# One fused audio-tower kernel: round two's results of token pairs 6 and 7 picked by TensorE from weight tables, and half of the shared experts moved forward

## The chip, the cores and the metric

The kernel runs on one core of one Trainium2 chip. The metric is device time in microseconds (us) of one execution. Five engines run their own instruction streams and meet at semaphores: TensorE (PE in the profile, its weight loads PEld), VectorE (DVE), ScalarE (ACT), GpSimd (POOL) and SyncE (SP), which here only issues DMAs.

## What is computed

Three layers on 64 batches x 16 positions = 1024 tokens of width 128, all in 32-bit floats:

```
h   = einsum("bg,egp->bep", x, weight * mask) + bias      # x: 64 x 5000, weight: 16 x 5000 x 128
h   = h + attention(layernorm(h))                         # 8 heads, causal over the 16 positions
xf  = layernorm(h)
s   = sigmoid(xf @ gate_w.T); top-2 of 64 experts; weights = s / sum(s) * 2.5
y_e = (silu(buf_e @ w1_e) * (buf_e @ w3_e)) @ w2_e         # tokens sent to expert e, at most 256
out = h + sum over the 2 chosen experts of weight * y + silu(xf @ sw1) * (xf @ sw3) @ sw2
```

The last term is the shared experts, which every token passes.

## The kernel before

The 1024 tokens are eight "pairs" of 128 (two positions of all 64 batches), numbered 0 to 7. The first stage streams 40 MB of weights through a ring of 12 buffers; VectorE and GpSimd multiply them by the mask, TensorE sums them (`sum_genes`, L843). Attention of pair j follows two pairs behind. After the last pair is summed, three pairs' attention is still to be finished; in the code that follows the loop `j, k, l` are the pairs 5, 6 and 7.

The experts work on slots. Tokens are scattered by indirect DMA (`scatter`, L486) into a DRAM table of expert inputs, SyncE loads that back (`load_slots`, L399), and 12 groups of 512 slot rows go through: `turn_xs` (transpose, L989 for round one, L993 for round two), `copy_xsT`, `up` (L1015), `silu` (with `copy`, L704/L705), `mid` (on GpSimd for groups 0 to 7, L508; on VectorE for 8 to 11, L1411), `turn_mid` (L1029), `copy_midT`, `down` (L1045), `copy_y` (L715) into `ys`. Groups 0 to 7 are round one (pairs 0 to 4), groups 8 to 11 round two (pairs 5 to 7; 32 slots per expert, 2048 rows). The last pair, 7, is not scattered: VectorE marks its slots (`mark_slots`, L1361/L1362, into `hot`) and TensorE adds its rows onto the transposed group with a 512-column matmul (`add_last`, L999).

`store_group` (L405, SyncE) writes each group's results to DRAM, and GpSimd's `gather` (L533, two indirect DMAs per pair, one for each of the two experts) reads every token's two rows back into `yg`: pairs 0 to 4 once all eight stores of round one have landed, pairs 5, 6, 7 once the four stores of round two have. `combine` (L1429, L1430) multiplies by the router's weights and adds them to `hres`, which by then holds h plus the shared experts' part. `write_out` (L430) stores the output, two DMAs for two pairs at a time, as `s_fin` counts up.

The router's weights of pairs 5 to 7 come from an exponential on ScalarE (`score_exp`, L725) and six small VectorE instructions (`weights`, L1417 to L1422), between `combine(3)` and `combine(4)`. The shared experts are done in two halves of 512 tokens after the last `down`: `shared_up` (two 512-column matmuls, L1056), `silu_shared` (L721), `shared_mid` (L1400), `shared_down` (four 128-column matmuls, L1064), `add_shared` (L1405).

Order is written out by hand: every engine has one program order, and a semaphore wait holds back all that stands behind it on that engine. On TensorE the stretch between the streaming loop and the experts is (L1067 on) `spin`s (dummy matmuls, L928), `turn_qk(k)`, `qkv(k)`, `turn_o(j)`, `values(k)`, `attend(j)`, `turn_xn(l)`, `turn_xs(0)`, `project(l)` (L865), spins and `turn_xs(1)`, `turn_xs(2)`, `up(0)`, `up(1)`, `turn_xs(3)`, `turn_qk(l)` (L869), `turn_xf(j)`, `turn_xs(4)`, `qkv(l)`, `gate(j)` and so on. On ScalarE: `copy_xnT(l)`, `copy_xsT(0)`, `copy_xsT(1)`, `square_qk(l)`, `norm_qk(l)`, `probs(k)`, `copy_xsT(2)`, `norm_xf(j)`, `copy_xsT(3)`, `turned_qk(l)` (L619), `copy_xfT(j)`, `silu(0)`, `heads_k(l)` (its last copy is L630), `silu(1)`, ... On VectorE `choose(j)` (L1336 to L1338), which waits for `gate(j)`, is followed by `multiply_keys(l)` (L1262), which waits for `heads_k(l)`.

Of the kernel before, what the change touches and what calls it, by code (L numbers as in the profile page):

```python
# [27 lines left out]
P = 128  # L28
# [20 lines left out]
GATHERED_EARLY = NCH1  # L49
# [50 lines left out]
def S_BANK(i):  # L100

    return ((1, 5, 7), (0, 2, 3))[i]
# [69 lines left out]
def tower_kernel(nc, x, tok_w, tok_b, tok_mask, W_dq, W_uq, W_qr, W_dkv, W_ukv, W_kr, W_o,  # L172
                 q_ln_g, q_ln_b, kv_ln_g, kv_ln_b, gate_w, w1, w3, w2, sw1, sw3, sw2, consts, masks, out):
    with ExitStack() as ctx:
# [8 lines left out]

        bank = [ctx.enter_context(nc.psum_tensor(f"bank{i}", [P, 512], F32)) for i in range(8)]
# [45 lines left out]
        wts = sb("wts", [P, NCH, 2])  # L230
        msel = sb("msel", [P, NCH, E], BF16)
# [21 lines left out]
        ssil, shs = ring_view(18304, 512), ring_view(18816, 512)  # L253

        hm = [mask[:, 256 * i:256 * (i + 1)].rearrange("p (i h) -> p i h", h=H) for i in range(2)]
        gt = [mask[:, 512 + 256 * i:768 + 256 * i].rearrange("p (i h) -> p i h", h=H) for i in range(2)]
        slot_iota, hot = xT[:, 0:M_SLOTS], prod[:, 0:M_SLOTS]
# [62 lines left out]
        s_iota, s_hot = sem("slot_iota_in"), sem("last_slots_marked")  # L320

# [31 lines left out]
        def _(sp):  # L353
            for j in range(NCH):
                for q in range(UNITS):
# [14 lines left out]
                    if j == 1 and q == UNITS - 1:  # L370
# [9 lines left out]
                        sp.dma_start(gw[0:E, :], gate_w).then_inc(s_tw, 16)  # L380
            sp.wait_ge(s_xTp, 5)
# [31 lines left out]
            load_w2(0, (0, WREM), (0, S))  # L413
            sp.dma_start(slot_iota, masks[:, M_W:M_W + M_SLOTS]).then_inc(s_iota, 16)
            sp.dma_start(sw13[:, 0, :], sw1).then_inc(s_sw, 16)
            sp.dma_start(sw13[:, 1, :], sw3).then_inc(s_sw, 16)
            sp.dma_start(sw2s, sw2).then_inc(s_sw, 16)
            for g in range(STORED_FIRST):
                store_group(g)
# [3 lines left out]
            for g in range(STORED_FIRST, GROUPS):  # L423
                store_group(g)
# [20 lines left out]
        def _(pool):  # L445
            pool.memset(half[:], -0.5).then_inc(s_pool, 1)
            pool.memset(zeros, 0.0).then_inc(s_zsrc, 1)
            pool.wait_ge(s_ones, 1)
# [67 lines left out]
            root_h2(j)  # L516
            mid(0)
            mid(1)
            mid(2)
# [6 lines left out]
            scatter(k)  # L526
            root_h2(l)
            mid(7)

# [8 lines left out]
            pool.wait_ge(s_slot, NCH - 1)  # L538
# [3 lines left out]
            pool.wait_ge(s_ys, GROUPS)  # L542
            for j in range(GATHERED_EARLY, NCH1):
                gather(j)
            pool.wait_ge(s_gidx, 1)
            pool.wait_ge(s_yout[1], 16 * (GROUPS - GROUPS1))
            for j in range(NCH1, NCH):
                gather(j)

        @block.scalar  # L550
        def _(act):
# [95 lines left out]
            def copy_xfT(j):  # L647
                act.wait_ge(s_xfT, j + 1)
                act.copy(xfT[:, P * j:P * j + P], bank[A_BANK(j)][:, 256:384]).then_inc(s_xfTs, 1)
# [72 lines left out]

            def score_exp(first, last):
                act.wait_ge(s_top, last)
                act.activation(ew[:, 0, first:last], top[:, first:last, 0:2], ACT.Exp, scale=-1.0).then_inc(s_exp, 1)  # L725
# [10 lines left out]
            copy_xnT(l)  # L736
            copy_xsT(0)
            copy_xsT(1)
            square_qk(l)
# [8 lines left out]
            heads_k(l)  # L748
            silu(1)
            heads_v(l)  # L750
            copy_oT(k)
# [37 lines left out]
            copy_xsT(9)  # L789
            copy_y(8)  # L790
            silu(9)
# [10 lines left out]
            silu_shared(0)  # L802
            silu_shared(1)
            score_exp(NCH1, NCH)
# [13 lines left out]
        def _(pe):  # L818
# [163 lines left out]
            def turn_xs(g):  # L982
# [37 lines left out]
            def turn_mid(g):  # L1020
                pe.wait_ge(s_hm, g + 1)
                if g >= 1:
                    pe.wait_ge(s_hT, g if g <= GROUPS1 else g - 1)
                if g == GROUPS1:
                    pe.wait_ge(s_kv, 2 * NCH)
# [7 lines left out]
            def down(g):  # L1033
# [3 lines left out]
                if g == 0:  # L1037
                    pe.wait_ge(s_w2, 16 * 4)
                if g >= 1:
# [10 lines left out]
            def shared_up(i):  # L1050

                if i == 0:
                    pe.wait_ge(s_sw, 48)
                    pe.wait_ge(s_hm, GROUPS)
# [500 lines left out]
```

## Time and profile before

| | us |
|---|---|
| runs | 239.67, 241.01, 241.49 (median 241.01) |
| the profiled execution | 241.4 |
| its span, first to last instruction | 239.7 |
| busy PE / DVE / ACT / POOL | 184.3 / 152.4 / 82.7 / 145.6 |
| granted TensorE clock, mean of the span | 0.953 |

Times of the trace count from the span's start. Busy shares are averages over a streaming stage (to some 157 us), a stretch of attention and experts side by side (to some 220 us) and a tail of DMAs, and say little of any one of them. "SPq" and "POOLq" are instructions that issue DMAs. A bracket at the end of a timeline row is the idle time of that engine just before it and what ended that.

### The profile page before, as it was taken

How to read it: one execution, taken by the hardware profiler on the slowest of the kernel's cores; microseconds unless marked ns; L12 is line 12 of the kernel's file. 1: busy time of each engine (PE TensorE's matmuls, PEld its weight loads, DVE VectorE, ACT ScalarE, POOL GpSimd, SP SyncE). 2: the span in 40 equal slices, each digit the busy share in tenths (PEclk: the TensorE clock that was granted, in tenths of full speed). 3: DMA queues.
4: the chain of work that ended last, by engine and by line, in shares of the span. 5: the costliest groups of instructions: out<-in, count | busy, mean ns of one | idle time of the engine just before them, and what ended most of it. 6: DMA issues, size and time to landing. Idle time of an engine off the chain costs nothing.

```text
span 239.7 us, 6216 instructions
## 1 busy us (share of the span) xinstructions
PE 184.3 (77%) x2549; PEld 154.8 (65%) x2549; DVE 152.4 (64%) x366; ACT 82.7 (35%) x245; POOL 145.6 (61%) x117
## 2 busy tenths in 40 slices
PE   0057969558989969979879789699997989999700
PEld 0056949457878958857758767588776767767400
DVE  0024384686497796897996994978999627410571
ACT  2005200003324324324133124136878744344400
POOL 3326469519998949879969949620161651375360
PEclk9999997977999989999999999999999999999975
DMA  6989999999999999999999999949901329234241
GB/s 220 290 311 417 362 419 384 346 421 415 421 413 417 420 418 420 414 427 418 403 408 228 234 218 191 153 87 303 263 0 44 115 68 296 68 98 121 71 112 35
DMA packets 32982, 65.12 MB, mean 272 GB/s; under 512 B 2874, under 2 KB 25367, under 8 KB 32375
## 3 DMA queue, kind: packets, MB, share of 16 engines
q1 hardware_dynamic: 31416, 59.47, 75.0%
q10 hardware_dynamic: 576, 3.26, 3.4%
q0 software_dynamic: 960, 1.97, 3.1%
q8 instruction: 21, 0.34, 0.6%
q14 instruction: 9, 0.07, 0.1%
HBM read 56.96 MB, written 7.73 MB: 270 GB/s over the span
## 4 chain that ended last, share of the span: by engine, by line
PE 32%; DVE 24%; DMA 18%; SPq 9%; ACT 6%; issue 5%; POOL 3%; POOLq 1%; DVEq 0%; ACTq 0%
DMA ring<-in_L_tok_weight_dram 16%; PE bank L843 10%; DVE ring L1241 5%; SPq L362 4%; DVE bank L1271 4%; PE bank L1045 3%; DVE prod L1262 3%; PE bank L1015 3%; DVE prod L1293 2%; DVE bank L1301 2%; SPq L368 2%; PE bank L993 2%; PE bank L999 2%; PE bank L928 2%; POOL rstd L455 2%
## 5 line engine op out<-in xcount | busy, mean ns | idle before, releaser
L466 POOL TENSOR_TENSOR ring<-ring,mask 128x896 f32<-128x896 f32 (+1 forms) x48 | 91.5, 1935 | 18.7 <-DMA ring<-in_L_tok_weight_dram 18.6
L843 PE MATMUL bank<-ring,xT 128*64 128x128 f32 x1248 | 84.3, 294 | 11.3 <-DVE ring L1241 8.0
L843 PEld LDWEIGHTS bank<-ring,xT 128*64 128x64 f32 x1248 | 76.4, 149 | 16.0 <-DVE ring L1241 12.8
L1241 DVE TENSOR_TENSOR ring<-ring,bank 128x1024 f32<-128x1024 f32 (+1 forms) x45 | 45.8, 1049 | 35.4 <-DMA ring<-in_L_tok_weight_dram 35.4
L455 POOL TENSOR_TENSOR rstd<-mv,half 128x1 f32<-128x1 f32 (+1 forms) x24 | 14.4, 603 | 32.4 <-DVE mv L1249 21.5
L533 POOL DMA_INDIRECT ring<-expert_outputs,slot_index x16 | 16.2, 1010 | 16.6 <-DMA expert_outputs<-ring 12.4
L824 PE MATMUL bank<-cst,w 64*128 64x64 f32 x39 | 5.3, 328 | 15.6 <-DMA w<-in_x_dram 14.8
L486 POOL DMA_INDIRECT expert_inputs<-xf,slot_index x14 | 14.3, 1022 | 4.3 <-issue 3.5
L508 POOL TENSOR_TENSOR mask<-ring,mask 128x256 f32<-128x256 f32 x8 | 7.5, 938 | 14.4 <-ACT ring L705 11.4
L824 PEld LDWEIGHTS bank<-cst,w 64*128 64x128 f32 x39 | 5.0, 219 | 15.7 <-issue 14.8
L579 ACT ACTIVATE offset<-shift,rstd 128x1 f32<-128x1 f32 x16 | 4.7, 292 | 25.1 <-POOL rstd L455 25.1
L1015 PE MATMUL bank<-w,ring 128*64 128x128 f32 (+1 forms) x256 | 12.9, 277 | 0.5 <-ACT ring L705 0.4
L1045 PE MATMUL bank<-w2p,ring 64*64 64x128 f32 (+1 forms) x256 | 12.8, 272 | 0.3 <-ACT ring L715 0.2
L1271 DVE TENSOR_REDUCE bank<-prod 128x16 f32<-128x288 f32 (+7 forms) x8 | 12.1, 1511 | 0.3
L1015 PEld LDWEIGHTS bank<-w,ring 128*64 128x64 f32 (+1 forms) x256 | 10.1, 123 | 2.6 <-ACT ring L696 1.1
L1045 PEld LDWEIGHTS bank<-w2p,ring 64*64 64x64 f32 (+1 forms) x256 | 10.2, 120 | 2.3 <-issue 1.2
L1293 DVE TENSOR_TENSOR prod<-vcat,bank 128x256 f32<-128x256 f32 (+7 forms) x8 | 10.8, 1344 | 0.0
L1301 DVE TENSOR_REDUCE bank<-prod 128x128 f32<-128x256 f32 (+7 forms) x8 | 10.6, 1321 | 0.0
L1262 DVE TENSOR_TENSOR prod<-kcat,bank 128x256 f32<-128x256 f32 (+5 forms) x6 | 6.5, 1089 | 4.8 <-ACT vcat L635 4.8
L1336 DVE MAX8 top<-bank 128x8 f32<-128x64 f32 x8 | 1.9, 232 | 12.0 <-PE bank L914 12.0
L715 ACT COPY ring<-bank 128x512 f32<-128x512 f32 x12 | 7.0, 585 | 7.0 <-PE bank L1045 7.0
L928 PE MATMUL bank<-cst 128*128 128x128 f32 x70 | 9.4, 279 | 0.0
(153 smaller groups left out, 297.4 us busy)
## 6 DMA issues: line engine op xcount, KB each, us to landing
ring<-in_L_tok_weight_dram SPq DMA_DIRECT2D x48, 832.0 KB, 13.5
expert_inputs<-w ACTq DMA_DIRECT2D x3, 1024.0 KB, 10.6
ring<-expert_inputs SPq DMA_DIRECT2D x6, 512.0 KB, 5.4
expert_outputs<-ring SPq DMA_DIRECT2D x12, 256.0 KB, 2.7
mask<-in_L_tok_mask_dram SPq DMA_DIRECT2D x3, 832.0 KB, 15.6
w<-in_x_dram SPq DMA_DIRECT2D x1, 1250.0 KB, 13.0
w2p<-in_L_ffn_w_dram SPq DMA_DIRECT2D x1, 1024.0 KB, 19.2
xT<-masks_dram SPq DMA_DIRECT2D x1, 1024.0 KB, 8.1
```

Of the source, the lines that this page charges most:

```text
L455: pool.tensor_tensor(rstd[:, a:b], mv[:, a:b, 1], half[:, 0:b - a], ALU.pow).then_inc(s_rstd, 1)
L466: pool.tensor_tensor(unit(j, q, SPLIT(q // 2), UC), unit(j, q, SPLIT(q // 2), UC), mask[:, (m + SPLIT(q // 2)) * D:(m + UC) * D], ALU.mult ...
L486: pool.indirect_dma_start(out=xs_dram[j // NCH1], out_offset=bass.IndirectOffsetOnAxis(ap=s_idx[:, j, k:k + 1], axis=0), in_=xf[:, j, :], ...
L533: pool.indirect_dma_start(out=yg[:, 2 * j + k, :], out_offset=None, in_=ys_dram[r], in_offset=bass.IndirectOffsetOnAxis(ap=s_idx[:, j, k:k ...
L843: last = pe.matmul(bank[0][64 * par:64 * par + 64, 0:D], xT[:, (UC * t + c) * B:(UC * t + c + 1) * B], unit(j, 2 * t + par, c, c + 1), sta ...
L928: pe.matmul(bank[where][:, 256:256 + P], ident, ident, start=True, stop=True)
L1015: last = pe.matmul(bank[U_BANK(g)][row:row + slots, tile * P:(tile + 1) * P], xsT[g % 2][:, n * slots:(n + 1) * slots], w13[:, EXPERT(g, n ...
L1045: last = pe.matmul(bank[Y_BANK(g)][row:row + slots, tile * D:(tile + 1) * D], hT[g % 2][H * par:H * par + H, tile * H + col:tile * H + col ...
L1241: dve.tensor_tensor(both(j, t, a, b), both(j, t, a, b), m.rearrange("p (u f) -> p u f", u=1).to_broadcast([P, 2, (b - a) * D]), ALU.mult). ...
L1271: then(dve.tensor_reduce(raw(j).rearrange("p (h s) -> p s h", h=NH), prod[:, 0:n * f].rearrange("p (s h d) -> p s h d", h=NH, d=DK), AX.X, ...
L1293: then(dve.tensor_tensor(prod[:, 0:n * D].rearrange("p (h d s) -> p h d s", d=DH, s=n), vcat[:, :, 0:n].rearrange("p (h d) s -> p h d s", ...
L1301: then(dve.tensor_reduce(o_raw(j), prod[:, 0:n * D].rearrange("p (f s) -> p f s", f=D), AX.X, ALU.add))
```

## The change

For pairs 6 and 7 (`LATE`) the two gathers are replaced. Two DRAM tables of 2048 x 128 floats (1 MB each) are zeroed by SyncE from a cleared tile (`no_picks`, set by GpSimd). ScalarE makes, per pair and expert choice, a diagonal matrix of the router's weights (`weight_rows`); GpSimd scatters its rows by the tokens' slot numbers (`scatter_picks`, two indirect DMAs per pair); SyncE loads each finished table into SBUF (`load_picks`); TensorE multiplies it with `ys` (`pick`, 16 matmuls per pair, summed in one bank), and VectorE adds the sum to `hres`. Pair 5 is gathered as before. `weights(5, 8)` moves in front of `mid(9)` on VectorE, and its exponential to GpSimd, as a power behind `mid(7)`.

The first half of the shared experts moves forward on all engines: `shared_up(0)` stands behind `project(l)`, with its own early copy of the two weight matrices (two 64 KB loads on SyncE between the loads of pair 1 and pair 2); its SiLU and a copy are on ScalarE around `silu(1)`, its product on GpSimd between `mid(1)` and `mid(2)`, `shared_down(0)` behind `rank_tokens(k)`, `add_shared(0)` on VectorE in front of `choose(l)`. `square_qk(l)` moves in front of `copy_xsT(0)`. Round two's `turn_xs` become transposes.

```diff
@@ SyncE
                         sp.dma_start(gw[0:E, :], gate_w).then_inc(s_tw, 16)
+                        sp.dma_start(sw13_first[:, 0, :], sw1).then_inc(s_sw1, 16)
+                        sp.dma_start(sw13_first[:, 1, :], sw3).then_inc(s_sw1, 16)
...
+            sp.wait_ge(s_nopick, 1)
+            for table in pick_dram:
+                sp.dma_start(table.rearrange("(p a r) t -> p a (r t)", p=P, a=2),
+                             no_picks.rearrange("p (a f) -> p a f", a=1).to_broadcast([P, 2, 1024])).then_inc(s_pickz, 16)
+            def load_picks(i):
+                sp.wait_ge(s_pscat[i], 32)
+                sp.dma_start(picks[i], pick_dram[i].rearrange("(i p) t -> p i t", p=P)).then_inc(s_pick[i], 16)
             for g in range(STORED_FIRST):
                 store_group(g)
             sp.wait_ge(s_scat[1], 16 * 2 * (NCH - 1 - NCH1))
             for i in range(GROUPS1 // 2, GROUPS // 2):
                 load_slots(1, i)
-            for g in range(STORED_FIRST, GROUPS):
+            for g in range(STORED_FIRST, GROUPS1):
+                store_group(g)
+            load_picks(0)
+            sp.wait_ge(s_prod, NCH)
+            load_picks(1)
+            for g in range(GROUPS1, GROUPS):
                 store_group(g)
@@ GpSimd
             root_h2(j)
+            pool.memset(no_picks, 0.0).then_inc(s_nopick, 1)
             mid(0)
             mid(1)
+            pool.wait_ge(s_ssil, 1)
+            pool.wait_ge(s_shg, 1)
+            pool.tensor_tensor(shs, ssil, shg, ALU.mult).then_inc(s_shs, 1)
             mid(2)
...
             mid(7)
+            pool.wait_ge(s_top, NCH)
+            pool.tensor_tensor(ew[:, 0, NCH1:, :], inv_e[:], top[:, NCH1:, 0:2], ALU.pow).then_inc(s_late_exp, 1)
+            def scatter_picks(j):
+                pool.wait_ge(s_diag, j - LATE[0] + 1)
+                pool.wait_ge(s_pickz, 16 * len(LATE))
...
+                for k in range(2):
+                    pool.indirect_dma_start(
+                        out=pick_dram[j - LATE[0]], out_offset=bass.IndirectOffsetOnAxis(ap=s_idx[:, j, k:k + 1], axis=0),
+                        in_=diag[:, j - LATE[0], k, :], in_offset=None, bounds_check=ROWS[1] - 1,
+                        oob_is_err=False).then_inc(s_pscat[j - LATE[0]], 16)
...
             pool.wait_ge(s_yout[0], 16 * GROUPS1)
-            for j in range(GATHERED_EARLY):
+            gather(0)
+            for j in LATE:
+                scatter_picks(j)
+            for j in range(1, NCH1):
                 gather(j)
...
             pool.wait_ge(s_yout[1], 16 * (GROUPS - GROUPS1))
-            for j in range(NCH1, NCH):
-                gather(j)
+            gather(NCH1)
@@ ScalarE
             copy_xnT(l)
+            square_qk(l)
             copy_xsT(0)
             copy_xsT(1)
-            square_qk(l)
...
             heads_k(l)
+            silu_shared(0)
             silu(1)
             heads_v(l)
+            copy_shared()
...
             copy_xsT(9)
+            weight_rows(NCH - 2)
             copy_y(8)
+            weight_rows(NCH - 1)
             silu(9)
...
-            silu_shared(0)
             silu_shared(1)
-            score_exp(NCH1, NCH)
@@ TensorE
-                        pe.matmul(bank[T_BANK(g)][:, i * P:(i + 1) * P], xs[:, PG * g + i, :], ident, start=i == 0, stop=False)
+                        pe.matmul(bank[T_BANK(g)][:, i * P:(i + 1) * P], xs[:, PG * g + i, :], ident, is_transpose=True,
+                                  start=i == 0, stop=False)
...
+            def pick(n):
+                pe.wait_ge(s_pick[n], 16)
+                for g in range(GROUPS1, GROUPS):
+                    if n == 0:
+                        pe.wait_ge(s_ys, g + 1)
+                    for i in range(PG):
+                        last = pe.matmul(bank[PICKED][:, n * D:(n + 1) * D], picks[n][:, PG * (g - GROUPS1) + i, :],
+                                         ys[:, PG * g + i, :], start=(n == 0 and g == GROUPS1 and i == 0),
+                                         stop=(n == len(LATE) - 1 and g == GROUPS - 1 and i == PG - 1))
+                last.then_inc(s_picked, 1)
...
             turn_xn(l)
+            spin(2, 7)
+            project(l)
+            shared_up(0)
             turn_xs(0)
-            project(l)
-            spin(3, 7)
+            spin(3, 1)
             turn_xs(1)
-            spin(3, 7)
+            spin(3, 1)
             turn_xs(2)
             up(0)
             up(1)
...
             rank_tokens(k)
+            shared_down(0)
             turn_mid(4)
...
             down(11)
-            shared_up(0)
             shared_up(1)
-            shared_down(0)
+            pick(0)
             shared_down(1)
+            pick(1)
@@ VectorE
             add_attended(l)
+            add_shared(0)
             choose(l)
...
             mark_slots(11)
+            mid(8)
             dve.tensor_copy(s_idx[:, l, :], last_slot[:]).then_inc(s_gidx, 1)
-            mid(8)
+            weights(NCH1, NCH)
             mid(9)
             mid(10)
             mid(11)
-            shared_mid(0)
-            add_shared(0)
             shared_mid(1)
             for j in range(4):
                 combine(j)
             add_shared(1)
-            weights(NCH1, NCH)
-            for j in range(4, NCH):
-                combine(j)
+            combine(4)
+            combine(5)
+            dve.wait_ge(s_picked, len(LATE))
+            dve.tensor_tensor(fin[:, LATE[0]:, :], hres[:, LATE[0]:, :],
+                              bank[PICKED][:, 0:len(LATE) * D].rearrange("p (j d) -> p j d", d=D), ALU.add).then_inc(s_fin, len(LATE))
```

## Rows read from the trace of the kernel before

**Rows 1.** The chain that ended last, from 218 us: start, length, what.

```profile
221.00 3.25 DMA expert_outputs<-ring
...
231.61 2.91 DMA ring<-expert_outputs,slot_index
...
234.93 0.35 DVE ring L1430
```

**Rows 2.** One line's instructions, L430 from 234 us: durations in ns, first and last start.

```profile
L430 SPq DMA_DIRECT2D out_dram<-ring x2: 596/603/610, 235.3 to 235.9; - x2
```

**Rows 3.** Timeline of TensorE, 152 to 182 us: start, length, line, operation.

```profile
164.76 0.52 PE L865 MATMUL bank<-wproj,xnT 128*128 128x149 f32 x2
...
167.71 1.97 PE L1015 MATMUL bank<-w,ring 128*64 128x128 f32 x32
169.71 0.66 PE L989 MATMUL bank<-cst,ring 128*128 128x128 f32 x4
170.20 0.27 PE L869 MATMUL bank<-cst,qkn 128*64 128x128 f32 x1
```

**Rows 4.** Timeline of TensorE, 182 to 240 us.

```profile
196.79 0.33 PE L910 MATMUL bank<-cst,xf 128*128 128x128 f32 x1 [0.25 <-ACT xf L582]
...
200.71 1.16 PE L993 MATMUL bank<-cst,ring 128*128 128x128 f32 x8
...
202.84 1.12 PE L999 MATMUL bank<-prod,xf 128*128 128x512 f32 x2
...
207.50 1.12 PE L999 MATMUL bank<-prod,xf 128*128 128x512 f32 x2
...
220.25 3.70 PE L1056 MATMUL bank<-xfT,ring 128*128 128x512 f32 x8
```

**Rows 5.** Timeline of ScalarE, 170 to 174 us, and its shared SiLU.

```profile
170.88 0.46 ACT L619 ACTIVATE cqT<-bank,lnp 64x128 f32<-64x128 f32 x1
...
172.10 1.28 ACT L705 ACT_TABLE_LOAD   x1
...
173.97 0.42 ACT L630 COPY kcat<-bank 128x256 f32<-128x256 f32 x1
...
222.27 0.60 ACT L721 ACTIVATE ring<-bank 128x512 f32<-128x512 f32 x1 [1.30 <-PE bank L1056]
```

**Rows 6.** Timeline of VectorE, three instructions.

```profile
174.42 2.31 DVE L1262 TENSOR_TENSOR prod<-kcat,qcat 128x2048 f32<-128x2048 f32 x1
...
202.04 0.75 DVE L1362 SCALAR_TENSOR_TENSOR prod<-xT,last_slot,prod 128x512 f32<-128x512 f32 x1
...
212.22 0.42 DVE L1411 TENSOR_TENSOR mask<-ring,bank 128x256 f32<-128x256 f32 x1 [5.44 <-ACT ring L705]
```

**Rows 7.** Timeline of GpSimd, four instructions.

```profile
173.86 0.73 POOL L508 TENSOR_TENSOR mask<-ring,mask 128x256 f32<-128x256 f32 x1 [4.39 <-ACT ring L705]
...
195.30 0.59 POOL L455 TENSOR_TENSOR rstd<-mv,half 128x1 f32<-128x1 f32 x1
...
225.09 1.00 POOL L533 DMA_INDIRECT ring<-expert_outputs,slot_index  x1 [5.10 <-DMA expert_outputs<-ring]
226.39 1.00 POOL L533 DMA_INDIRECT ring<-expert_outputs,slot_index  x1 [0.31 <-issue]
```

**Rows 8.** Windows: five engines' busy us (instructions), TensorE clock, DMA share, GB/s.

```profile
36.00:38.00 2.00, 1.74 (x18) 1.74 (x20) 0.81 (x2) 0.00 (x0) 2.00 (x2) 0.59 1.02 423
...
176.00:180.00 4.00, 4.00 (x72) 3.36 (x70) 3.97 (x3) 3.11 (x7) 2.54 (x3) 1.00 0.00 0
...
202.00:204.00 2.00, 2.00 (x20) 1.32 (x17) 1.93 (x4) 0.59 (x1) 0.00 (x0) 1.00 1.07 321
```

**Rows 9.** Landing of GpSimd's L486 scatters issued at 193.00 and 194.32.

```profile
DMA to landing us min/median/max: 2.2/2.3/2.3
```

**Rows 10.** Landing of SyncE's first L399 load of round two (512 KB, issued 196.57).

```profile
DMA to landing us min/median/max: 4.0/4.0/4.0
```

**Rows 11.** DMA issues: shared weights, issued at 166.16 to 167.12, behind a 1 MB load.

```profile
ring<-in_L_ffn_sw_dram SPq DMA_DIRECT2D x3, 64.0 KB, 7.3
```

More of the change, by code:

```diff
@@ L48 @@
 CAP = 256
-GATHERED_EARLY = NCH1
+LATE = range(NCH1 + 1, NCH)
 WREM = 16
@@ L100, in S_BANK @@
 def S_BANK(i):
-    return ((1, 5, 7), (0, 2, 3))[i]
+    return ((4, 7, 3), (0, 2, 0))[i]
+PICKED = 4
 def A_BANK(j):
@@ L253, in tower_kernel @@
         ssil, shs = ring_view(18304, 512), ring_view(18816, 512)
+        shg = ring_view(17280, 512)
+        sw13_first = xfT[:, (NCH - 2) * P:NCH * P].rearrange("p (a d) -> p a d", a=2)
         hm = [mask[:, 256 * i:256 * (i + 1)].rearrange("p (i h) -> p i h", h=H) for i in range(2)]
         gt = [mask[:, 512 + 256 * i:768 + 256 * i].rearrange("p (i h) -> p i h", h=H) for i in range(2)]
+        diag = mask[:, 1024:1024 + 2 * len(LATE) * P].rearrange("p (j k t) -> p j k t", k=2, t=P)
+        no_picks = mask[:, 1792:1792 + 1024]
+        picks = [v.rearrange("p (i t) -> p i t", t=P)
+                 for v in (mask[:, 2816:2816 + ROWS[1]], kcat[:].rearrange("p s h d -> p (s h d)")[:, 0:ROWS[1]])]
         slot_iota, hot = xT[:, 0:M_SLOTS], prod[:, 0:M_SLOTS]
@@ L320, in tower_kernel @@
         s_iota, s_hot = sem("slot_iota_in"), sem("last_slots_marked")
+        s_inv, s_late_exp, s_wts, s_diag = sem("inverse_e_set"), sem("late_top2_exp"), sem("weights"), sem("weight_rows")
+        s_nopick, s_pickz = sem("pick_zeros"), sem("picks_zeroed")
+        s_pscat, s_pick = [sem(f"picks_scattered{j}") for j in LATE], [sem(f"picks_in{j}") for j in LATE]
+        s_picked, s_shg, s_sw1 = sem("round_two_picked"), sem("shared_gate_copied"), sem("shared_w_in_first")
         s_sh1, s_ssil, s_shs, s_sh2, s_shared = (sem("shared_up"), sem("shared_silu"), sem("shared_mid"),
@@ L721, in silu_shared, with copy_shared, weight_rows @@
                 act.activation(ssil, bank[S_BANK(i)[0]][:], ACT.Silu).then_inc(s_ssil, 1)
+            def copy_shared():
+                act.copy(shg, bank[S_BANK(0)[1]][:]).then_inc(s_shg, 1)
+            def weight_rows(j):
+                act.wait_ge(s_wts, 2)
+                act.wait_ge(s_pmask, UNITS * NCH)
+                act.activation(diag[:, j - LATE[0], 0, :], ident, ACT.Identity, scale=wts[:, j, 0:1])
+                act.activation(diag[:, j - LATE[0], 1, :], ident, ACT.Identity, scale=wts[:, j, 1:2]).then_inc(s_diag, 1)
             def score_exp(first, last):
@@ L1038, in down @@
                     pe.wait_ge(s_w2, 16 * 4)
+                    pe.wait_ge(s_shg, 1)
                 if g >= 1:
@@ L1052, in shared_up @@
                 if i == 0:
+                    pe.wait_ge(s_sw1, 32)
+                    pe.wait_ge(s_xfTs, 4)
+                else:
                     pe.wait_ge(s_sw, 48)
-                    pe.wait_ge(s_hm, GROUPS)
+                    pe.wait_ge(s_xsT, GROUPS)
+                    pe.wait_ge(s_xfTs, NCH)
+                up_weights = sw13 if i else sw13_first
                 for a in range(2):
-                    last = pe.matmul(bank[S_BANK(i)[a]][:], sw13[:, a, :], xfT[:, 512 * i:512 * i + 512], start=True, stop=True)
+                    last = pe.matmul(bank[S_BANK(i)[a]][:], up_weights[:, a, :], xfT[:, 512 * i:512 * i + 512], start=True, stop=True)
                 last.then_inc(s_sh1, 1)
@@ L1415, in weights @@
                 n = slice(first, last)
-                dve.wait_ge(s_exp, 1 if first == 0 else 2)
+                if first == 0:
+                    dve.wait_ge(s_exp, 1)
+                else:
+                    dve.wait_ge(s_late_exp, 1)
                 then(dve.tensor_scalar(ew[:, 1, n], ew[:, 0, n], 1.0, None, ALU.add))
@@ L1420, in weights @@
                 then(dve.reciprocal(ew[:, 0, n, 1], ew[:, 0, n, 0]))
-                for i in range(2):
-                    mark(dve.scalar_tensor_tensor(wts[:, n, i], ew[:, 2, n, i], ROUTE_SCALE, ew[:, 0, n, 1], ALU.mult, ALU.mult))
-                marked()
+                then(dve.scalar_tensor_tensor(wts[:, n, 0], ew[:, 2, n, 0], ROUTE_SCALE, ew[:, 0, n, 1], ALU.mult, ALU.mult))
+                dve.scalar_tensor_tensor(wts[:, n, 1], ew[:, 2, n, 1], ROUTE_SCALE, ew[:, 0, n, 1],
+                                         ALU.mult, ALU.mult).then_inc(s_wts, 1)
+                if first == 0:
+                    dve.wait_ge(s_wts, 1)
             def combine(j):
```

29 lines of the change are left out of this document (18 added, 11 removed).

## The prediction

> **What bounds the kernel now.** I read the chain that ended last first. Its tail is no engine's work: the last copy of results, the store of group 11 (3.25 us), six gathers issued one after another, the last one's landing (2.91 us) and two VectorE instructions that end at 235.28 [rows 1]. TensorE had finished its last `down` at 220.25 [rows 4]. So 15.0 us lie between the end of the expert work and the last sum, and this is what the change attacks. After it come two output stores, at 235.3 and 235.9 [rows 2], and the span ends at 239.7; the execution took 241.4, 0.4 above the runs' median.
>
> Next I read each engine's timeline where the change adds work. From 164.76 to 170.20 TensorE issues `project(l)`, spins, three `turn_xs`, two `up`s without a gap that matters [rows 3]. ScalarE takes 3.51 us from `turned_qk(l)` at 170.88 to the end of `heads_k(l)` at 174.39, a table load of 1.28 in it [rows 5]. VectorE starts `multiply_keys(l)` at 174.42 with no idle time in its row: it was busy until then, and its input came at the same moment [rows 6]. Neither side has slack, and all of pair 7's routing follows. In round two TensorE is bound by its own order but for a few waits on VectorE.
>
> **A: two early loads of 64 KB.** They stand among the weight loads, where the DMA engines are full at 423 GB/s [rows 8]: 131 KB / 423 = 0.3 us. Bounds 0 and 0.6 (twice that, if they also break up the order of the big loads). I take 0.3.
>
> **B: the first shared half at 165 us.** `shared_up(0)` is half of the L1056 row: 3.70 / 2 = 1.85 [rows 4]. `turn_xs(0)`, 0.49 from start to start [rows 3], filled the wait for `xnT` before and now comes behind it; spins fill that wait instead. So `turn_qk(l)` goes from 170.20 to 172.55. The earlier `square_qk(l)` hides GpSimd's root, but TensorE's order decides here, not ScalarE's: `copy_xsT` follows `turn_xs`. ScalarE's 3.51 us then run from 173.25 to 176.75, and `multiply_keys(l)` starts at 176.8: +2.4. ScalarE also has a SiLU (0.60) and a copy of that size around `silu(1)` [rows 5], which puts TensorE's and ScalarE's side 0.45 further. I take +2.85; bounds 0 (if that stretch were waiting anyway) and 3.5. GpSimd's product (two times 0.73) and its clearing of 1024 columns lie in its waits, 4.39 us long in front of `mid(0)` [rows 7]; without cover they would add about 1.5 each. The product waits for `copy_shared`, and `mid(2)` stands behind it; `turn_mid(2)`, which needs that, is later by as much. `turn_mid(0)` and `down(0)` wait for the SiLU and the copy, which are over by then. The zeroing of both tables, 2.1 MB, lands while the DMA engines stand still [rows 8].
>
> **C: `shared_down(0)`.** Four matmuls with fresh weights, about 1.1 like the four of an L993 group [rows 4]. Walking the order behind it, `turn_mid(4)`, `mid(6)`, the scatter of pair 6 and `root_h2(l)` (195.30, right behind that scatter [rows 7]) slip by 0.4, `turn_xf(l)` (196.79, which waited 0.25 [rows 4]) by 0.7, `up(7)` and `gate(l)` by 0.45. I take +0.45; bounds 0 and 1.1.
>
> **D: round two's transposes.** An L993 group takes 1.1, a transposed one 0.49 [rows 3, 4]: 0.6 each, 2.4 for four. Most of it meets a wait. Behind the first, `add_last(8)` at 202.84 [rows 4] waits for `mark_slots(8)`, which ends at 202.79 [rows 6]: nothing. Behind the second, `up(8)` waits for the copy of what `add_last(8)` wrote: 0.15. Behind the third, `turn_mid(8)` waits for VectorE's `mid(8)`, which moves one small instruction forward: nothing more. The fourth is whole. I take -0.7; bounds -2.4 and -0.3. The Trainium skill ("TensorE: Matmul & The Clock Gate", Terms) calls the transpose mode four times faster for FP32; the rows show 2.2 times, the sum goes by them, and by the page's factor it would be about 0.2 lower.
>
> So the last `down` ends at 220.25 + 0.3 + 2.85 + 0.45 - 0.7 = 223.15.
>
> **E: the two weight rows and `weights`.** VectorE's six small instructions go into its 5.44 us of waiting before `mid(9)` [rows 6]. The diagonals stand behind `copy_xsT(9)`, which follows `add_last(9)`: 207.50 [rows 4] plus 1.06, plus 3.45 of shift, plus a copy of 0.6, plus two ScalarE instructions of 0.45 (between the copies of 256 and 512 columns, 0.42 and 0.60 [rows 5]) = 213.5. They delay `copy_y(8)` and `silu(9)` by half a us, which `add_last(10)` and `add_last(11)` cover.
>
> **F: the tail.** GpSimd's first indirect DMA comes 0.84 after what it waited for (224.25 and 225.09), the next ones 1.30 apart [rows 1, 7]. Four scatters start at 214.35, 215.65, 216.95 and 218.25 and land 2.3 later [rows 9], so table 6 is complete at 218.0, table 7 at 220.6. Then come the eight gathers of pairs 1 to 4: GpSimd is free at 229.95. While SyncE waits for table 6 the store of group 8 stands behind that wait, which costs nothing by itself: only pair 5 needs it.
> SyncE's order is table 6, table 7, then the stores of groups 8 to 11. Loads of 512-byte rows ran at 321 GB/s with the DMA engines full [rows 8]; 512 KB alone lands after 4.0 [rows 10], of which 1.6 is data. Three 64 KB loads issued behind a 1 MB load took 7.3 to land [rows 11]: one queue is worked off in order. So data flow from 220.4; table 6 is in at 223.7, table 7 at 227. The stores are 1 MB more (3.3), the gathers beside them 0.5 MB (1.6): the last store lands at 231.8.
> TensorE meanwhile: `shared_up(1)` to 225.0, `pick(0)` (16 matmuls of the L993 shape, 4 x 1.09 = 4.36) to 229.4, `shared_down(1)` to 230.5, `pick(1)` to 234.8, both tables there in time. VectorE's last sum would be done at 235.4.
> Pair 5 is later: its gathers start at 232.65 and 233.95, land at 236.85 (2.91 [rows 1]), and the two VectorE instructions end at 237.6. Before, the output stores of pairs 4 and 5 were long gone when 6 and 7 came; now all four follow one another, two times 0.6 more [rows 2].
> Last sum and queue: 237.6 + 1.2 + 4.4 = 243.2 against 239.7, +3.5. On 241.4 that is 244.9, and 0.4 less at the level of the median: **244.5**. The tail by itself, counted from the last `down`, shrinks from 15.0 to 14.45 and loses that again in the output queue. Bounds of F: the last store lands between 227 (its own 3.25 behind the copy) and 233 (DMA at 280 GB/s).
>
> **The rivals.**
> R1, the picks end the kernel. If the stores of round two aren't held up behind the tables, GpSimd is the next bound: free at 229.95, pair 5 lands at 234.15 and is summed at 234.9; TensorE's picks give 235.4. The output queue costs 0.8, so the span ends at 240.5: +0.8 and, at the median's level, **241.8**, no change. It decides at one point: whether the store of group 11 has landed by about 229. For it speaks that stores landed in 3.25 [rows 1]; against it the 7.3 of the small loads.
> R2, the early half is free. If VectorE had some other wait at 174, B falls to 0 and the rest stands: 244.5 - 2.85 = **241.7**. Against it: no idle time in the row of 174.42.
> R3, both: 241.8 - 2.85 = **238.9**, the one case near a gain.
> R4, the tables come late and TensorE waits for them. If scatters of 512-byte rows into DRAM and 1 MB loads beside the gathers take half as long again, `pick(1)` ends 2.5 us later and the stores with it: **247**.
>
> **How the numbers follow.** The forecast has 0.55, R1 0.17, R2 0.10, R3 0.10, R4 0.08. The forecast's own spread is 243 to 246.5, from the bounds of B (0.6 upward) and of F. One per cent, 2.4 us, is about what a measurement of this kernel can tell from no change: below 238.6 is faster, above 243.4 slower. Slower: 0.43 of the forecast and R4's 0.07 make 0.50. Faster: half of R3 and 0.07 for what of the three first cases falls that low if several bounds go the good way at once, 0.12. Between: 0.38. The range runs from 239.8, which leaves out most of R3, to 247.0, which leaves out half of R4.
>
> **What would show it.** Right: `turn_qk(l)` near 172.6 and `multiply_keys(l)` near 176.8, with an idle bracket that names ScalarE; the last `down` near 223; GpSimd's last two gathers after 231, waiting for a store; the picks over before them. Wrong: `multiply_keys(l)` at 174.4 (then B was free), GpSimd going from pair 4 to pair 5 without a wait (then the queue didn't matter), or TensorE idle in front of a pick (R4).

## The result, and the profile after

The change is slower: 247.55 us (median of 4 runs, 246.58 to 248.12) against 241.25, ratio 1.026 (95% interval 1.019 to 1.033). The interval leaves open whether it is slower by more than 2%. The forecast was 244.5 with a range to 247.0: right in its direction, 3.05 too low. The profiled execution took 247.49, its span is 245.8.

The chain that ended last, of the kernel after, from 218 us (start, length, what):

```profile
218.25 6.75 DMA picks<-mask,slot_index
...
225.14 0.72 SPq L443
...
225.91 2.06 SPq L423
...
230.25 4.72 DMA expert_outputs<-ring
...
235.72 0.99 POOL ring L588
...
237.02 2.59 DMA ring<-expert_outputs,slot_index
...
240.66 0.04 DVE ring L1577
```

In [rows 1] the chain went from the store of group 11 through six gathers. It now goes through a scatter of 64 KB, 22 us before the last sum: the fourth one, issued at 218.25, lands after 6.75 us. SyncE waits for it, issues table 7's load at 225.14 and only then the four stores. The last of these lands at 234.97, pair 5 is gathered behind it, and the last sum is done at 240.70.

GpSimd's timeline shows the same as a bracket of six us in front of pair 5's first gather. In [rows 7] GpSimd waited there too, 5.10 us, but only until 225.09, and six gathers followed; now the wait ends at 235.72, and two follow:

```profile
214.34 1.02 POOL L579 DMA_INDIRECT picks<-mask,slot_index  x1 [0.94 <-ACT mask L785]
...
218.25 0.99 POOL L579 DMA_INDIRECT picks<-mask,slot_index  x1 [0.30 <-issue]
...
228.72 1.00 POOL L588 DMA_INDIRECT ring<-expert_outputs,slot_index  x1 [0.30 <-issue]
235.72 0.99 POOL L588 DMA_INDIRECT ring<-expert_outputs,slot_index  x1 [6.00 <-DMA expert_outputs<-ring]
237.02 0.99 POOL L588 DMA_INDIRECT ring<-expert_outputs,slot_index  x1 [0.30 <-issue]
```

SyncE's timeline, and the windows of the tail (columns as in [rows 8]: engines' busy us, TensorE clock, DMA share, GB/s):

```profile
218.04 0.73 SPq L443 DMA_DIRECT2D mask<-picks  x1
225.14 0.72 SPq L443 DMA_DIRECT2D kcat<-picks  x1
225.91 4.88 SPq L423 DMA_DIRECT2D expert_outputs<-ring  x4
230.84 12.11 SPq L462 DMA_DIRECT2D out_dram<-ring  x8
```

```profile
221.00:224.00 3.00, 2.99 (x86) 2.42 (x83) 0.00 (x0) 1.84 (x5) 2.39 (x3) 1.00 1.06 325
224.00:226.50 2.50, 2.50 (x15) 1.78 (x14) 0.39 (x1) 0.82 (x2) 1.89 (x3) 1.00 0.21 54
226.50:230.00 3.50, 3.40 (x31) 3.21 (x29) 2.17 (x7) 0.00 (x0) 2.60 (x3) 1.00 0.99 270
230.00:235.00 5.00, 3.46 (x31) 3.46 (x32) 2.01 (x5) 0.00 (x0) 0.00 (x0) 1.00 1.09 324
```

Between the two tables the DMA engines stand nearly still for 2.5 us (share 0.21), though the results of all four groups have been copied by 224.23 (the last `copy_y`, on ScalarE): their stores stand behind SyncE's wait.

```profile
223.64 0.59 ACT L769 COPY ring<-bank 128x512 f32<-128x512 f32 x1 [0.33 <-PE bank L1115]
```

TensorE, then VectorE's `multiply_keys(l)` and the end of ScalarE's `heads_k(l)`, to be held against [rows 3, 4, 5, 6]:

```profile
173.24 0.27 PE L935 MATMUL bank<-cst,qkn 128*64 128x128 f32 x1
...
178.62 0.62 PE L1082 MATMUL bank<-w,ring 128*64 128x128 f32 x7 [0.48 <-ACT ring L759]
...
223.46 1.98 PE L1131 MATMUL bank<-xfT,ring 128*128 128x512 f32 x4
225.28 3.73 PE L1151 MATMUL bank<-ring,mask 128*128 128x128 f32 x32
228.85 1.06 PE L1141 MATMUL bank<-ring 128*128 128x128 f32 x8
231.54 3.84 PE L1151 MATMUL bank<-ring,kcat 128*128 128x128 f32 x32 [1.63 <-DMA kcat<-picks]
```

```profile
176.71 0.23 DVE L1428 MAX8 top<-bank 128x8 f32<-128x64 f32 x1 [1.27 <-PE bank L980]
...
177.46 2.31 DVE L1354 TENSOR_TENSOR prod<-kcat,qcat 128x2048 f32<-128x2048 f32 x1
```

```profile
177.01 0.42 ACT L682 COPY kcat<-bank 128x256 f32<-128x256 f32 x1
```

`turn_qk(l)` moved from 170.20 to 173.24 and the last `down` from 220.25 to 223.46. Both contain 0.76 by which the attention of pair 5 came later in this execution; between the fourteen profiled executions that moment lies anywhere from 152.8 to 155.5. Below, "from the mark" is counted from pair 5's exponential on ScalarE, the first row here before and the second after:

```profile
154.44 0.25 ACT L641 ACTIVATE bank<-sc 128x96 f32<-128x96 f32 x1 [4.20 <-DVE sc L1284]
155.20 0.25 ACT L693 ACTIVATE bank<-sc 128x96 f32<-128x96 f32 x1 [4.19 <-DVE sc L1376]
```

From there on, traces with the same order agree to 0.05 us as long as TensorE's clock doesn't fall: the last `down` ends 68.24 to 68.26 from the mark in the change, e1, e2, e5 and e9, where it was 65.81 before. `multiply_keys(l)` starts 22.26 from the mark instead of 19.98.

### The profile page after: what moved, and what is told of

The parts are those of the page before. It is cut to its first block, busy times and chain, and to the rows that moved or that the text cites. A ratio compares the mean times of both kernels' runs of the same rounds, so it can differ in the third digit from the quotient of the medians.

```text
span 245.8 us, 6340 instructions
## 1 busy us (share of the span) xinstructions
PE 188.5 (77%) x2601; PEld 157.7 (64%) x2601; DVE 151.3 (62%) x362; ACT 82.7 (34%) x248; POOL 149.2 (61%) x121
## 4 chain that ended last, share of the span: by engine, by line
PE 35%; DVE 20%; DMA 15%; SPq 10%; ACT 9%; issue 6%; POOL 2%; DVEq 0%; ACTq 0%; POOLq 0%
PE bank L909 12%; DMA ring<-in_L_tok_weight_dram 9%; DVE ring L1333 5%; SPq L378 4%; PE bank L1082 3%; DVE bank L1363 3%; DMA picks<-mask,slot_index 3%; DVE prod L1354 2%; PE bank L994 2%; PE bank L1115 2%; DMA expert_outputs<-ring 2%; SPq L384 2%; SPq L423 2%; DVE prod L1385 2%; PE bank L1098 2%
## 5 line engine op out<-in xcount | busy, mean ns | idle before, releaser
L909 PE MATMUL bank<-ring,xT 128*64 128x128 f32 x1248 | 81.8, 288 | 13.2 <-DVE ring L1333 7.8
L909 PEld LDWEIGHTS bank<-ring,xT 128*64 128x64 f32 x1248 | 73.6, 145 | 18.3 <-DVE ring L1333 12.5
L588 POOL DMA_INDIRECT ring<-expert_outputs,slot_index x12 | 12.2, 1013 | 15.0 <-DMA expert_outputs<-ring 11.9
L541 POOL TENSOR_TENSOR mask<-ring,mask 128x256 f32<-128x256 f32 x8 | 6.9, 864 | 17.0 <-ACT ring L759 13.8
L994 PE MATMUL bank<-cst 128*128 128x128 f32 x74 | 10.0, 279 | 0.0
L1098 PE MATMUL bank<-cst,mask 64*64 64x64 f32 x192 | 7.9, 223 | 1.9 <-ACT ring L765 1.3
L994 PEld LDWEIGHTS bank<-cst 128*128 128x128 f32 x74 | 9.0, 192 | 0.5 <-issue 0.5
```

The costliest lines, as they stand in the source:

```text
L588: pool.indirect_dma_start(out=yg[:, 2 * j + k, :], out_offset=None, in_=ys_dram[r], in_offset=bass.IndirectOffsetOnAxis(ap=s_idx[:, j, k:k ...
L909: last = pe.matmul(bank[0][64 * par:64 * par + 64, 0:D], xT[:, (UC * t + c) * B:(UC * t + c + 1) * B], unit(j, 2 * t + par, c, c + 1), sta ...
L994: pe.matmul(bank[where][:, 256:256 + P], ident, ident, start=True, stop=True)
L1098: last = pe.matmul(bank[M_BANK(g)][rows, i * H:(i + 1) * H], hm[g % 2][rows, i, :], ident[rows, rows], start=True, stop=True)
```

## The experiments

| | what | median us | ratio to before (95%) |
|---|---|---|---|
| e1 | both tables loaded behind the fourth scatter | 248.9 (one run) | |
| e2 | stores ahead of table 7 | 247.16 | 1.024 (1.014 to 1.035) |
| e3 | picks without the early half | 246.20 | 1.018 (1.011 to 1.024) |
| e4 | early half without picks and transposes | 244.60 | 1.012 (1.007 to 1.017) |
| e5 | e2, TensorE kept busy | 246.22 | 1.023 (1.017 to 1.029) |
| e6 | pair 7 alone picked | 241.26 | 1.001 (0.997 to 1.004) |
| e7 | transposes alone | 240.31 | 0.996 (0.993 to 0.999) |
| e8 | e3 with e5's order | 245.41 | 1.017 (1.011 to 1.022) |
| e9 | half tables | 243.53 | 1.011 (1.007 to 1.016) |
| e10 | half tables, stores ahead | 242.45 | 1.006 (1.002 to 1.009) |
| e11 | e6, table and pick last | 240.47 | 0.996 (0.992 to 1.000) |
| e12 | early loads alone | 241.98 | 1.003 (1.000 to 1.007) |

**e1: is it table 6's load that holds the fourth scatter?**

```diff
+            sp.wait_ge(s_pscat[1], 32)
             load_picks(0)
             sp.wait_ge(s_prod, NCH)
             load_picks(1)
```

> Open is why table 7 was complete only at 225.0, its last scatter (issued 218.25) landing after 6.8 us where the three before took 2.2 to 2.3. Theory: the 1 MB load of table 6, issued at 218.04, stood in the DMA engines. Here SyncE waits for both tables before it loads either, so nothing stands in the way: the scatter lands after 2.3 to 2.6, the loads are issued near 220.7 and 221.4, table 6 is in at 227, table 7 at 230.5, the last store lands near 234 and the span is 244.5 to 246 (little is won, since the same 3.7 MB follow). Rival: the fourth scatter is slow by itself (it is the last before eight gathers on one queue); then it lands at 225 again, both loads start there and the span grows by 3 to 5 us.

With no table's load in the DMA engines the fourth scatter landed 2.85 us after its issue instead of 6.75 (from the chain of e1):

```profile
217.04 2.85 DMA picks<-mask,slot_index
```

The end didn't follow: both tables and then the stores now came one behind another from 219.96, the last store landed at 235.2 again, and the span of 247.1 is longer than I had expected. TensorE's timeline of e1 shows a second loss:

```profile
222.25 1.98 PE L1132 MATMUL bank<-xfT,ring 128*128 128x512 f32 x4
227.82 6.62 PE L1152 MATMUL bank<-ring,mask 128*128 128x128 f32 x32 [3.59 <-DMA mask<-picks]
```

`pick(0)` came after 3.59 us in which TensorE did nothing, and took 6.62 instead of 3.73: the granted clock was 0.50, that is 1.2 GHz, from 228 to 232. This didn't set the end, though: `pick(1)` was over at 238.92, and pair 5's gather landed at 240.94.

**e2: does the stores' place in the queue cost the rest?**

```diff
             load_picks(0)
             sp.wait_ge(s_prod, NCH)
-            load_picks(1)
             for g in range(GROUPS1, GROUPS):
                 store_group(g)
+            load_picks(1)
```

> SyncE issues the four stores of round two between the loads of table 6 and table 7. Theory (the order of SyncE's queue set the end): store 11 lands by 228.5 in place of 235.0, GpSimd goes from pair 4 to pair 5 near 230 without a wait for a store, pair 5 is summed by 235, table 7 lands near 232 and the second pick ends the kernel at 236 to 236.5: span 241 to 242, 4 to 5 us less than with the whole change. Rival (the sum of the bytes set the end, in whatever order): last store and table both near 235, span 245 to 246.

The profiled execution took 244.02. GpSimd ran through without a wait, its last gathers at 230.47 and 231.76, five us earlier than in the change; now the last sum waits for table 7, which is loaded last and takes 7.8 us to land. The fourth scatter again landed with table 6's load, after 6.36 us (load: 6.6). From e2's chain, and VectorE's last sum:

```profile
218.59 6.36 DMA picks<-mask,slot_index
...
225.15 7.80 DMA kcat<-picks
```

```profile
236.93 0.42 DVE L1577 TENSOR_TENSOR ring<-hres,bank 128x256 f32<-128x256 f32 x1 [0.90 <-PE bank L1151]
```

The other executions took 245.43, 248.9 and 249.34: two of the four lie 2.1 and 3.5 below the change's median, but little is left of it in e2's own. I put this down to TensorE's clock in the 2.75 us before `pick(1)`, and tried that in e5.

**e3 and e4: the two halves of the change apart.** e3 puts the first shared half back to where it stood before; e4 has that half early, with the two loads, and neither picks nor transposes. Both keep a part of the change that its cut above leaves out: SyncE loads two of the shared weights ahead of the last load of the experts' `w2`. The cut here is TensorE's part of e3, against the change.

```diff
+            turn_xs(0)
             project(l)
-            shared_up(0)
-            turn_xs(0)
...
+            shared_up(0)
             shared_up(1)
             pick(0)
+            shared_down(0)
             shared_down(1)
             pick(1)
```

> The change with the first half of the shared experts back behind the last down product and without its early loads. Theory (B and C of the prediction, 2.8 and 0.4, and the early loads 0.3 to 0.8): VectorE starts the keys' product of pair 7 at 174.4 again, the last down product ends near 219.7 in place of 223.5, and the tail, still set by the stores, moves with it: span 242 to 242.5. Rival (the early half was free): last down near 223, span 245 to 246.

> The kernel before with the early half alone: its early loads, its place on all engines, nothing picked, no transposes, the router's exponential where it was. Theory: the last down product ends 3.5 to 3.9 later, at 223.8 to 224.2, and the tail (store, six gathers) follows unchanged: span 243 to 243.7, 3.3 to 4 us slower than before. Rival (free): 239.7.

e4 costs 3.0 us (244.6 against 241.64 on the same chip). In its trace `multiply_keys(l)` starts 22.25 from the mark, like in the change: term B is the early half's and nothing else's. Its last `down`, at 224.18, and its span, 243.1, lie where I expected them, but in part by luck: the mark came 0.66 earlier than before, and about 1.5 us of that trace go to a fall of TensorE's clock (the last `down` ends 70.4 from the mark, where 68.3 of the change and 0.6 for the missing transposes make 68.9). In e3 `multiply_keys(l)` starts at 20.48, so the shift is gone but for 0.5, yet the ratio is only 0.8 points below the change's, and the two intervals overlap. For the profiled execution the windows of e3 tell why:

```profile
172.00:174.00 2.00, 1.58 (x20) 1.08 (x19) 1.93 (x6) 1.99 (x7) 0.52 (x1) 0.97 0.97 391
174.00:176.00 2.00, 1.94 (x18) 1.94 (x20) 2.00 (x2) 1.27 (x5) 1.56 (x2) 0.50 1.03 410
176.00:178.00 2.00, 2.00 (x20) 1.44 (x18) 1.97 (x3) 1.07 (x3) 0.94 (x1) 0.50 1.02 420
178.00:180.00 2.00, 2.00 (x28) 1.88 (x26) 1.90 (x3) 0.44 (x2) 0.73 (x1) 0.50 0.27 107
```

TensorE ran at 1.2 GHz for about seven us, `up(2)` took 1.92 instead of 1.09, and the last `down` ended 68.25 from the mark, as late as in the change. The same fall, 3 to 7 us long, stands in the profiles of e4, e8, e10 and e12, and not in those of before, after, e1, e2, e5, e6, e7, e9 and e11. No part of the change goes with it; what does is told in the last section.

**e5 and e8: TensorE kept busy ahead of the second pick.** e5 is e2 with the spins; e8 is e3 with the order of e2 and the spins.

```diff
             shared_down(1)
+            spin(24, 3)
             pick(1)
```

> The change with table 7's load behind the four stores (as in e2), and 24 dummy matmuls of 128 columns in front of pick(1), so that TensorE is not idle while table 7 comes in. If the spread of e2 (244.0 and 245.4, but also 248.9 and 249.3) comes from TensorE falling to its lower clock in that wait (pick(1) 3.84 us at full clock, 3.7 more at half of it), all executions should lie between 243.5 and 245.5, and pick(1) still starts near 233 (24 times 0.11 is 2.65 of the 2.75 us that it waited). Rival: the spread comes from elsewhere (the clock in the attention stretch, or the DMA queues); then executions near 249 stay and the median stays above 246.5.

> e5 with the first shared half back behind the last down, as in before. Theory: at full clock in the attention stretch the last down ends 3 us earlier than in the change, and shared_up(0) and shared_down(0), 2.9 us, fill the time in which TensorE waits for the tables; the last sum is limited by table 7 (landing near 230 instead of 233) and by the gathers of pair 5 (issued near 228): 240.5 to 242.5. Rival: the clock falls in the attention stretch as in e3 (then 243.5 to 245), or the table and not the early half sets the end (then as e5, 244).

Both missed, first of all by an error of mine: a spin is two matmuls in the trace, and the 24 took 5.5 us instead of the 2.65 that I had counted. TensorE's timeline of e5:

```profile
228.94 5.52 PE L994 MATMUL bank<-cst 128*128 128x128 f32 x48
234.30 3.74 PE L1151 MATMUL bank<-ring,kcat 128*128 128x128 f32 x32
```

The second pick started 79.9 from the mark, in e2 77.5: the spins outlasted the table, which landed at the same 77.5 in e5, by 2.4. No execution of e5 reached 249, but they still spread from 244.75 to 248.06, and the granted clock averaged over the span was at least 0.965 in each. So the clock isn't all of e2's spread; the rest is open. With the 2.4 taken off, e5's median would be 243.8, an estimate from these two traces: the order of the queue would then be worth between 3 and 4 of the change's 6.3 us. No run shows it without the spins and without e2's spread. In e8 the spins ended at 235.2, and table 7's load had been issued at 220.74: the spins set its end, and it says nothing on the early half.

**e9 and e10: half of each table.**

```diff
-                sp.dma_start(picks[i], pick_dram[i].rearrange(...
+                sp.dma_start(picks[i][:, 0:8, :], pick_dram[i][0:8 * P].rearrange(...
...
-                for g in range(GROUPS1, GROUPS):
+                for g in range(GROUPS1, GROUPS1 + 2):
```

> The change, but only the first half of each table is loaded (512 KB) and picked (groups 8 and 9; the rows of groups 10 and 11 are left out of the sum). Theory: the fourth scatter lands with the end of table 6's load, so it now lands after about 4.3 us instead of 6.8; table 7's load is issued near 222.5 instead of 225.1, the stores follow at once, the last one lands near 230, GpSimd goes on to pair 5 near 230.3 with hardly a wait, and the last sum is done near 235: span 240.5, time 242 to 243, some 5 below the change. Rival: the fourth scatter's landing has nothing to do with that load's size and stays near 6.8; then the stores are still issued behind 225 and only 1 MB of data less is in front of them: last store 232.5, time 244.5 to 245.5.

> As e9, with table 7's half load behind the four stores. If the volume in the DMA engines sets the tail (3.5 MB in the change, 2.5 MB here), this is 3 below e2 and e5: 242 to 243.5, and no better than e9. Rival: the order of the queue matters more than the volume; then it is 1.5 or more below e9.

SyncE's and GpSimd's timelines of e9, and how table 6's half was issued and landed:

```profile
217.68 0.36 SPq L443 DMA_DIRECT2D mask<-picks  x1
222.97 0.36 SPq L443 DMA_DIRECT2D kcat<-picks  x1
223.37 3.64 SPq L423 DMA_DIRECT2D expert_outputs<-ring  x4
```

```profile
217.95 0.98 POOL L579 DMA_INDIRECT picks<-mask,slot_index  x1 [0.30 <-issue]
...
231.59 0.99 POOL L588 DMA_INDIRECT ring<-expert_outputs,slot_index  x1 [2.20 <-DMA expert_outputs<-ring]
```

```profile
mask<-picks SPq DMA_DIRECT2D x1, 512.0 KB, 5.0
```

Table 6's load landed after 5.0 us instead of 6.8, and the fourth scatter with it: SyncE came past its wait 5.0 us after the scatter's issue, not 6.9. The wait ahead of pair 5 shrank from 6.00 to 2.20, and the ratio fell from 1.026 to 1.011, some 3.5 us. That is the theory's mechanism at two thirds of its size; e9's 243.53 lies 0.5 above the range that I had given. How the 3.5 us divide between the scatter's earlier landing and the 1 MB less behind it isn't shown. e10 lies in its range, but 1.1 below e9, where the theory had it no better and the rival 1.5 better: at half the volume the order of the queue is worth about one us, though the two intervals overlap. Its profile has the clock's fall as well, which cost about 1.5 us there.

**e6 and e11: one table instead of two.** e6 is e3 with pair 7 alone picked, and its table's load behind the store of group 8; e11 moves load and pick to the end. The cut is of e11, against the change; in e6 the load stands behind `store_group(GROUPS1)` and `pick(0)` in front of `shared_down(0)`.

```diff
-LATE = range(NCH1 + 1, NCH)
+LATE = range(NCH1 + 2, NCH)
...
-            load_picks(0)
-            sp.wait_ge(s_prod, NCH)
-            load_picks(1)
             for g in range(GROUPS1, GROUPS):
                 store_group(g)
+            load_picks(0)
...
+            shared_up(0)
             shared_up(1)
+            shared_down(0)
+            shared_down(1)
             pick(0)
-            shared_down(1)
-            pick(1)
```

> Only pair 7 is picked by TensorE (one table of 1 MB, two scatters, sixteen matmuls); pairs 5 and 6 are gathered; both halves of the shared experts stay behind the last down; the table's load stands behind the store of group 8. Theory (the tail of before is six gathers behind the store of group 11, 1.30 apart; the tables cost through 3.5 MB in one stretch): now four gathers stand behind that store, the last one is issued near 228.7, lands 2.9 later, the last sum is done near 232.5 instead of 235.3, and the time is 238.5 to 239.5, that is 2 to 3 below before. Rival 1: the clock falls in the attention stretch as in e3 and takes 2.9 back: 241.5 to 242.5. Rival 2: the 1 MB load still delays the stores of groups 9 to 11 by its own 3.3 us of data: the four gathers start at 228 and the time is 242 or more.

> e6 with the table's load behind all four stores of round two and its sixteen matmuls behind both shared_down. Theory: e6 lost its gain because the 1 MB load held the store of group 11 for 1.7 us and because pick(0) held shared_down(0), for which VectorE's sums waited. Without both, GpSimd starts the last four gathers right behind the first ten (near 225.1 instead of 226.6), the last lands near 232, and the sum is done near 233 instead of 235.1: 239 to 239.8 beside 241.3 before (ratio 0.990 to 0.994). Rival: the table's load now lands with the gathers and pick(0) or the gathers come late by as much: 240.5 to 241.5.

e6 went its second rival's way, if not as far: 241.26 where the rival had 242 or more. Its four last gathers started at 226.59 behind a wait of 1.82 for the store, and VectorE, held by the late `shared_down(0)`, was busy without a gap from 228.84 to the last sum at 235.06. In e11 GpSimd no longer waits, but the chain that ended last shows what came in its place, as its rival had it:

```profile
222.08 7.33 DMA mask<-picks
...
229.45 3.85 PE bank L1132 x32
```

The table's load shares the DMA engines with the gathers and lands after 7.33. e11 is 0.4% below before, no more than the transposes give alone (e7); so the one pick, too, returned nothing that can be told.

**e7 and e12: two small terms alone.**

```diff
-  pe.matmul(bank[T_BANK(g)][:, i * P:(i + 1) * P], xs[:, PG * g + i, :], ident, start=i == 0, stop=False)
+  pe.matmul(bank[T_BANK(g)][:, i * P:(i + 1) * P], xs[:, PG * g + i, :], ident, is_transpose=True,
+            start=i == 0, stop=False)
```

> Before, with round two's four turn_xs groups as transposes and nothing else. The prediction's term D: four groups 0.6 shorter each, of which waits on VectorE swallow all but 0.7: ratio 0.997, and the last down 0.7 earlier relative to pair 5's exponential (65.1 us instead of 65.8). Rival: they are whole on the path (2.4 us, ratio 0.990), or nothing is left of them in the time because the stores and gathers behind are not TensorE's (ratio 1.000).

> Before with the two early 64 KB loads alone (their data go unused). The prediction's term A: 131 KB at 423 GB/s, 0.3 us, ratio 1.001, bounds 0 and 0.6. Rival: they break up the order of the big loads and cost 1 us or more (ratio 1.004 or above).

e7 gains 0.4% (1.0 us, interval 0.3 to 1.8); the last `down` ends 65.21 from the mark instead of 65.81. This is the one part of the change that pays, and, with e11, the fastest kernel seen. e12 adds to before the two loads, and one wait that keeps their target free. It costs 0.3% (0.8 us, 0 to 1.6), between the theory's 0.1% and the rival's 0.4%. Its profile has TensorE waiting 1.24 us for the slot rows of the first group and the clock's fall, in an execution that was the slowest of its twelve, so the time and not that trace speaks for the term.

## Why the prediction came out as it did

| step | predicted | measured |
|---|---|---|
| A, early loads | +0.3 | +0.8, 0 to 1.6 (e12) |
| B, `multiply_keys(l)` / `up(2)` from the mark | +2.4 / +2.85 | +2.28 / +2.77 |
| B and C, `add_last(8)` from the mark | +3.3 | +3.11 |
| A to C in time | +3.6 | +3.0, 1.7 to 4.2 (e4; clock's fall in its trace) |
| D, from `add_last(8)` to the last `down` | -0.7 | -0.66; -0.60 alone (e7) |
| E, first and fourth scatter at | 214.35, 218.25 | 214.34, 218.25 |
| F, fourth scatter lands after | 2.3 | 6.75 |
| F, last store lands at | 231.8 | 234.97 |
| F, last sum behind the last `down` | 14.45 | 17.24 |
| F, from the last sum to the end | 5.6 | 5.1 |

A to D agree within what the runs can tell. E's moments agree to 0.01 us, but that is luck: 0.76 of the measured ones is the later mark of this execution, and from the mark the scatters came 0.8 earlier than counted (0.5 with A's 0.3 put ahead of the mark). The early half isn't free (R2 falls): a row without idle time in front of it, [rows 6], was the right sign that the stretch has no slack, and VectorE's 1.27 us of waiting in front of `choose(j)` is the bracket that the text asked for, with TensorE as the releaser and not ScalarE, whose side comes ready at the same moment: `heads_k(l)` ends at 177.43, `multiply_keys(l)` starts at 177.46. R1 falls with the six us in front of pair 5. The mechanism of F was right: stores stuck behind the tables' loads, and pair 5 behind the stores.

What failed is one term of F: "Four scatters start at 214.35, 215.65, 216.95 and 218.25 and land 2.3 later". Three did. The fourth is issued 0.21 us behind table 6's load of 1 MB, and landed with it. I had taken 2.3 from scatters beside which the DMA engines were less than half busy [rows 9] (share 0.46 from 192 to 194 us and 0.18 from 194 to 196), although the same step had just put a 1 MB load beside this one, and although I used the small loads that took 7.3 behind a large one [rows 11], but for SyncE's own queue alone. That a transfer of another queue waits likewise is shown by four runs: behind 1 MB 6.75 us (6.36 in e2), behind 512 KB about 4.9 (e9), with no table's load beside it 2.85 (e1). Had the two queues been served turn by turn, one would expect it about as soon behind the half as behind the whole. The change's own gathers say the same: one issued at 219.54 took 5.1 us, one at 222.21 took 3.5, landing at 224.6 and 225.7 around table 6's end at 224.8, and one issued at 226.11, beside table 7, took 5.6.

The Trainium skill ("DMA: Bandwidth & Descriptors", Queues, rings and completion order) has two sentences on this: each DMA engine takes turns between the queues, packet by packet, and a transfer's count on its semaphore lands only after every earlier write of that engine, across its queues. The first alone would have the scatter through early, against the 6.75 and 4.9 here; the second goes the way of these rows, without saying by how much. That they are the cause no run here shows.

The miss carries through almost whole. Table 7's load was issued 4.5 us later than counted (225.14, not near 220.6), the DMA engines stood nearly still for 2.5 of them, and at some 300 GB/s instead of 321 the rest took about 0.5 longer: the last store landed 3.2 late, the last sum 2.8 more behind the last `down`, and 0.3 of the start and -0.5 of the output queue make the span 2.6 longer than forecast. The other 0.4 of the 3.05 is what the forecast took off for the level of the median; after the change the profiled execution lies at the median. With the term went "both tables there in time": R4 had the right place (the tables late, TensorE waiting 1.63 before `pick(1)`, 247) but named bandwidth as the reason and got a chance of 0.08.

If the parts add up, the picks as a whole, e4 and e7 taken off the change, cost 1.8% (1.026 - 1.012 + 0.004), 4.3 us with some 2 either way from the three intervals; F had them at 0.65.

## What to carry to other kernels

Take a transfer's landing time only together with what is in the DMA engines beside it. Before taking a duration from a quiet row, write down which large transfer of any queue is issued just ahead of it; here a scatter of 64 KB landed with the table's load issued 0.2 to 0.3 us before it, at 1 MB as at 512 KB. A wait for such a small transfer on a queue that also carries finished results holds these back as well. Stores that have their data are better off in front of it: in e2 pair 5's gathers came five us earlier for it, but table 7, now last, set the end, and the median gained little. And here two gathers of 64 KB, 1.30 apart, were cheap beside the table of 1 MB, 6.4 us and more to land, that was loaded to avoid them.

## What the hardware showed beyond that

TensorE's clock fell to 1.2 GHz for 3 to 7 us between 173 and 182 us in five of the fourteen traces, and cost 1.4 to 3.1 us there (the last `down` from the mark, beside traces with the same order). These five are the ones in which the mark came earliest, at 152.75 to 153.78; in the other nine it came at 153.99 to 155.52. So an early start of the attention stretch and the fall go together in these traces. No run moved the mark by itself, and what starts the fall stays open. The kernel before may have the like in some executions: of 23 on one chip, the four with mean granted clocks of 0.935 to 0.937 took 242.05 to 244.12, while the four fastest (239.34 to 240.07) had 0.956 to 0.968; where in the span they lost it, their numbers don't say. In the tail `pick(0)` of e1 ran at that lower clock after 3.59 us without work, and `pick(1)` didn't after 1.63 (the change) and 2.75 us (e2), 3.84 us long both times.
